# 128 rows per gather, node one-hots on ScalarE, earlier logits, and a mixing stage without GpSimd

## Chip, core and metric

The kernel runs on one core of a Trainium2 chip. The metric is the device time of one execution in microseconds (us). A core has a matrix engine (TensorE, PE in the rows, its weight loads PEld), a vector engine (VectorE, DVE), a scalar engine (ScalarE, ACT), GpSimd (POOL) and SyncE (SP). Each runs its own instruction queue in order and meets the others through semaphores. Everything is float32.

## What is computed

A two-layer graph block on 3125 nodes of 256 features and 50000 edges, sorted by destination. Cut to what matters here:

```python
# layer 0: two attention convolutions with one head (GATv2)
h      = leaky_relu(xl[src] + xr[dst] + edge_attr @ We, 0.2)
logits = h @ att
ex     = exp(logits - segment_max(logits, dst)[dst])
out    = segment_sum(xl[src] * (ex / segment_sum(ex, dst)[dst])[:, None], dst)

# layer 1: one attention convolution with eight heads
e   = leaky_relu(eh[src] + ee + et[dst], 0.2)
ex  = exp(e - segment_max(e, dst)[dst])
rst = segment_sum(ft[src] * (ex / segment_sum(ex, dst)[dst])[:, :, None], dst)

# layer 1: linear mixing, N = 3125
k2 = l2_normalize(k*k / (sum(k*k) + 1e-7), over nodes)
q2 = l2_normalize(q*q / (sum(q*q) + 1e-7), over features)
out = (v + q2 @ (k2.T @ v) / sqrt(N)) @ W_out + b_out
```

Beside them stand a four-layer linear attention, two mixtures of experts, and norms, which the change leaves alone.

## The kernel before

Nodes lie in 25 tiles of P = 125 partitions, edges in steps of 125. The function `messages` makes one convolution. It is called three times: calls 1 and 2 have one head (`one` is true), call 3 has eight. Its 432 steps form 27 groups of G = 16, and buffers over groups form a ring of RB = 3.

For each step it fetches the source rows of 125 edges with one indirect DMA from GpSimd (`gather`, L656), in four blocks of four steps; block b of group g waits until PE has summed the same block of group g - 3 (L653), whose rows it overwrites. A one-hot matrix `oht` (node by edge) gives PE the destination's term: SyncE loads a row of tile-relative numbers into all partitions (L673), and `node_hots` (L694) turns the 125 x 2000 block of a group into ones and zeros with one VectorE comparison. PE multiplies it with the node rows and, with one head, adds the gathered rows through an identity (`score`, L862 and L866; L872 with eight heads). VectorE makes the `relu` and its sum (L701, one head) and the `logits` (L709, or L718 to L722), running maxima (`own_maxima`, `carries`, `maxima`), and the exponent's `arguments` (L760 to L766); ScalarE makes the exponentials (L950), with one head the scaling of the gathered rows (L971), and the other one-hot `oh` (edge by node), step by step through a ring of four (L960, L964). With eight heads VectorE scales the rows (`scale`, L773). PE sums them with `oh` into one of three banks (`aggregate`, L908), and VectorE adds the bank to the accumulator (`combine`, L792), which it rescales once per group (`rescale`, L783 or L786).

Every engine runs a `body(j, ...)` per group, written out by hand. In body j the logits of group j get their maxima and exponentials, group j + 1 is scored, and group j - 1 is summed and combined. VectorE goes through k = 0 to 15: each k combines one step, with the maxima at k = 1, 3 and 5, the arguments at k = 8, the node one-hots of group j + 2 and the indices of group j + 3 at k = 9, the scaling at 12 to 15 (eight heads), and the logits of group j + 1 at the end. PE goes through eight pairs p, each with two scores and two sums, and five asides on p = 0 to 4: `turn_logits` (L879), `turn_ends` (L884, L885), `turn_carries` (L891), `turn_run` (L897), `spread_factor` (L902). ScalarE takes, per group, the exponentials, the scaling, and `edge_hots` of the next group (L960, L964).

`square_mix` makes the linear mixing. In its first loop over the 25 tiles PE projects, ScalarE squares, VectorE evicts and normalises (L1825 to L1843) and closes the convolution of call 3: it multiplies the accumulator (L1846) and adds it to `x2` (L1849). GpSimd adds the two column sums `ksum` and `k2sum` (L1635, L1644) and the bias `shift` to `x2` (L1640). In its second loop PE makes the output products (L1704) and VectorE adds them to `x2` (L1867).

## Time and profile before

| | us |
|---|---|
| median of 3 runs (lowest, highest) | 5218.85 (5206.32, 5223.74) |
| the profiled execution | 5204.3 |
| its span, from first to last instruction | 5202.5 |
| call 1 of `messages`, first to last gather | 1613.2 to 2291.2 |
| call 2 | 2537.1 to 3212.1 |
| call 3 | 3903.3 to 4594.3 |
| `square_mix` | about 4640 to 4812 |

| engine | busy us | share of the span |
|---|---|---|
| PE | 4340.8 | 83% |
| DVE | 2738.6 | 53% |
| ACT | 2171.7 | 42% |
| POOL | 2022.1 | 39% |

A row of a group names line, engine, operation, output and inputs with their shapes, and the count of instructions; then their busy time, the mean of one, and the idle time of the engine just ahead of them with what ended it. A PE operation in float32 is issued as two instructions, so sixteen steps are 32 rows. Idle time put down to "issue" is ended by nothing that the profile shows. The chain of work that ended last reaches only over the last part of the program and doesn't touch these stages, so they are read by windows.

### The profile page before, as it was taken

The page shows a single profiled execution, that of the slowest core. Times are in us where ns is not written, and L with a number is a line of the kernel's source. Part 1 is how long each engine was busy: PE and PEld are TensorE (multiplying, and loading weights), DVE is VectorE, ACT ScalarE, POOL GpSimd, SP SyncE. Part 2 cuts the span into 40 slices and gives each one's busy share as a digit, 9 for nine tenths or more (in the row PEclk, how much of TensorE's full clock was granted, in tenths as well). Part 3 has the DMA queues.
Part 4 walks back from the last instruction along what each step waited for, and adds up shares of the span by engine and source line. Part 5 has one row for each costly group of instructions (what it writes and reads, how often), then busy time and mean ns, then how long its engine had stood idle before and what let it go on. Part 6 is the DMA issues. An engine that isn't in the chain of part 4 may idle for free. (4 is left out here: it accounts for less than half of the span.)

```text
span 5202.5 us, 73734 instructions
## 1 busy us (share of the span) xinstructions
PE 4340.8 (83%) x21745; PEld 3584.4 (69%) x21746; DVE 2738.6 (53%) x8592; ACT 2171.7 (42%) x6651; POOL 2022.1 (39%) x1623
## 2 busy tenths in 40 slices
PE   9589999999995899988699998749936888878694
PEld 8478879788794777765577776438935666655694
DVE  2263452634523666764366666363355777766324
ACT  2243434434442666652366666122243333333222
POOL 0000000000004888840488885106618888833141
PEclk9789999999997999996899999659965666579697
DMA  5510000000005555530455553472267656620613
GB/s 141 145 52 10 18 10 1 18 10 18 1 21 124 126 126 125 125 88 19 98 125 127 129 125 83 93 219 68 63 146 151 136 135 135 134 67 25 202 36 87
DMA packets 364626, 463.24 MB, mean 89 GB/s; under 512 B 166429, under 2 KB 296743, under 8 KB 363790
## 3 DMA queue, kind: packets, MB, share of 16 engines
q1 hardware_dynamic: 172546, 258.16, 19.5%
q0 software_dynamic: 191744, 200.92, 17.5%
q8 instruction: 172, 2.82, 0.2%
q14 instruction: 164, 1.34, 0.1%
HBM read 396.61 MB, written 60.67 MB: 88 GB/s over the span
## 5 line engine op out<-in xcount | busy, mean ns | idle before, releaser
L656 POOL DMA_INDIRECT msg_rows<-tab_d,msg_cur x1296 | 1649.9, 1273 | 1762.8 <-DVE msg_cur L142 1368.7
L908 PE MATMUL msg_agp<-msg_rows,msg_oh 125*125 125x261 f32 (+2 forms) x2592 | 849.5, 457 | 14.3 <-DVE ga_acc L792 10.7
L908 PEld LDWEIGHTS msg_agp<-msg_rows,msg_oh 125*125 125x125 f32 x2592 | 549.0, 223 | 125.1 <-DVE ga_acc L792 18.2
L862 PE MATMUL msg_zp<-g_xr,msg_oht 127*125 x1728 | 544.3, 396 | 64.5 <-DVE msg_oht L696 64.2
L866 PE MATMUL msg_zp<-msg_rows,c_ident 125*125 125x256 f32 x1728 | 528.9, 387 | 81.9 <-DMA msg_rows<-tab_d,msg_cur 81.5
L701 DVE SCALAR_TENSOR_TENSOR msg_hid<-msg_zp,g_att 125x256 f32<-125x256 f32 x864 | 360.8, 420 | 334.3 <-PE msg_zp L866 329.5
L960 ACT ACTIVATE msg_dist<-c_iota,c_rel 125x125 f32<-125x125 f32 x1296 | 493.3, 387 | 49.7 <-PEq L3077 34.7
L964 ACT ACTIVATE msg_oh<-msg_dist,c_ones 125x125 f32<-125x125 f32 x1296 | 493.5, 387 | 0.0
L950 ACT ACTIVATE msg_ex<-msg_arg 125x16 f32<-125x16 f32 (+1 forms) x81 | 20.0, 247 | 984.9 <-DVE msg_delta L766 984.9
L866 PEld LDWEIGHTS msg_zp<-msg_rows,c_ident 125*125 125x125 f32 x1728 | 323.9, 190 | 153.7 <-DMA msg_rows<-tab_d,msg_cur 103.6
L792 DVE TENSOR_TENSOR gv_acc<-gv_acc,msg_agp 125x261 f32 (+1 forms) x864 | 364.4, 422 | 72.4 <-PE msg_agp L908 64.9
L862 PEld LDWEIGHTS msg_zp<-g_xr,msg_oht 127*125 127x125 f32 x1728 | 306.8, 189 | 117.1 <-issue 65.4
L1240 PE MATMUL mix_pb<-mix_ht,mix_w 128*128 128x125 f32 x3200 | 373.5, 275 | 0.0
L1249 PE MATMUL mix_pc<-mix_w,mix_ut 128*125 128x256 f32 x1600 | 361.8, 380 | 7.1 <-ACT mix_ut L1381 7.1
L1240 PEld LDWEIGHTS mix_pb<-mix_ht,mix_w 128*128 128x128 f32 x3200 | 365.6, 192 | 0.4
L971 ACT ACTIVATE msg_rows<-msg_rows,msg_ex 125x257 f32<-125x257 f32 x864 | 354.2, 497 | 1.8
L1516 DVE TENSOR_TENSOR mix_t<-mix_pc,mix_b 125x256 f32<-125x256 f32 x100 | 42.5, 425 | 543.5 <-PE mix_pc L1249 543.5
L1249 PEld LDWEIGHTS mix_pc<-mix_w,mix_ut 128*125 128x125 f32 x1600 | 292.9, 188 | 48.0 <-issue 8.3
L1202 PE MATMUL mix_pb<-mix_wp,mix_ht 128*125 128x256 f32 x1200 | 284.8, 389 | 4.3 <-ACT mix_ht L1321 4.3
L792 DVE TENSOR_TENSOR ga_acc<-ga_acc,msg_agp 125x264 f32 x432 | 184.2, 426 | 161.7 <-PE msg_agp L908 145.4
L1202 PEld LDWEIGHTS mix_pb<-mix_wp,mix_ht 128*125 128x125 f32 x1200 | 223.8, 193 | 36.9 <-issue 5.6
L1321 ACT ACTIVATE mix_ht<-mix_pa,mix_gb 128x125 f32<-128x125 f32 x208 | 83.0, 451 | 368.8 <-PE mix_pa L1191 368.8
(552 smaller groups left out, 7221.1 us busy)
## 6 DMA issues: line engine op xcount, KB each, us to landing
msg_oht<-rel_d SPq DMA_DIRECT2D x81, 875.0 KB
msg_rows<-tab_d,msg_cur POOLq DMA_INDIRECT x1296, 3.9
pl_raw<-in_edge_attr SPq DMA_DIRECT2D x25, 448.0 KB
msg_pens<-pen_d SPq DMA_DIRECT2D x270, 31.2 KB
msg_oht<-rel_d SPq DMA_DIRECT2D x81, 101.6 KB
mix_w<-in_L_mix_W SPq DMA_DIRECT2D x8, 1024.0 KB
m0w_wr<-in_L_ffn_w SPq DMA_DIRECT2D x16, 512.0 KB
m0w_w2r<-in_L_ffn_w SPq DMA_DIRECT2D x16, 512.0 KB
```

The lines of the kernel that those rows point to most:

```text
L656: nc.gpsimd.indirect_dma_start(out=rows[:, q, k, :], out_offset=None, in_=table, in_offset=bass.IndirectOffsetOnAxis(ap=cur[:, q, k:k + 1] ...
L701: last = nc.vector.scalar_tensor_tensor(out=hid[:, k, :], in0=zp[:, pair_bank(u, k // 2), (k % 2) * D:(k % 2 + 1) * D], scalar=0.0, in1=at ...
L792: nc.vector.tensor_tensor(a_t, a_t, agp[:, sum_bank(u, k), 0:AW], ALU.add).then_inc(combined.sem, 1)
L862: nc.tensor.matmul(z, hots, d_t, start=True, stop=False)
L866: last = nc.tensor.matmul(z, c.ident[0:P, 0:P], rows[:, u % RB, k, 0:D], start=False, stop=True)
L908: nc.tensor.matmul(agp[:, sum_bank(u, k), 0:AW], oh[:, u % RB, k, :], rows[:, u % RB, k, 0:AW], start=True, stop=True).then_inc(summed.sem, 1)
L960: nc.scalar.activation(dist[:, k % 4, :], c.iota[0:P, 0:P], ACT.Abs, scale=-1.0, bias=c.rel[:, bass.ds(g * G + k, 1)]).then_inc(dist_ready ...
L964: last = nc.scalar.activation(oh[:, u % RB, k - 1, :], dist[:, (k - 1) % 4, :], ACT.Relu, scale=-1.0, bias=c.ones[0:P, 0:1])
L971: nc.scalar.activation(r, r, ACT.Copy, scale=ex[:, u % RB, k:k + 1]).then_inc(scaled.sem, 1)
L1202: last = nc.tensor.matmul(pb[bank][0:P, lo:lo + D], ht[:, t % HR, kc, :], wp[:, w, kc, :], start=(kc == 0), stop=(kc == 1))
L1240: last = nc.tensor.matmul(out, w1[:, kc, f * 128:(f + 1) * 128], ht[:, t % HR, kc, :], start=(kc == 0), stop=(kc == 1))
L1249: last = nc.tensor.matmul(pc[t % 2][0:P, 0:D], ut[:, t % 2, f, :], w2[:, f, :], start=(f == 0), stop=(f == FC - 1))
```

## The change

The diff has five parts.

1. A gather fetches 128 rows: `rows` and `cur` get 128 partitions, and so does `src_s`, whose rows 125 to 127 stay zero, so that three more copies of table row 0 land in partitions that nothing reads.
2. `node_hots` moves from VectorE to ScalarE and becomes two activations over the 125 x 2000 block, |part - x| and relu(1 - |.|), the second of which waits for the first. It stands at the head of ScalarE's body, for group j + 2.
3. The `rescale` of the one-head calls takes its factor as a second tensor input and not as a scalar.
4. With eight heads PE makes all 16 scores of group j + 1 in pairs 0 to 3, four to a pair, and VectorE makes the logits of group j + 1 at k = 10 and not after k = 15.
5. `square_mix` has no GpSimd block. VectorE makes the two column sums in the first loop; the additions to `x2` (accumulator, then `shift`) move to the second loop, two tiles ahead of their use.

```diff
-        rows = st.sb("rows", [P, RB, G, TW])
-        cur = st.sb("cur", [P, RB, G], I32)
+        rows_all = st.sb("rows", [ROWS, RB, G, TW])
+        rows = rows_all[0:P]
+        cur = st.sb("cur", [ROWS, RB, G], I32)
...
-                            nc.gpsimd.indirect_dma_start(out=rows[:, q, k, :], out_offset=None, in_=table,
+                            nc.gpsimd.indirect_dma_start(out=rows_all[:, q, k, :], out_offset=None, in_=table,
...
-                def node_hots(g, u, lap):
-                    dve.wait_ge(hots_landed[u % RB].sem, hots_landed[u % RB].at(lap * hots_in + hots_in))
-                    nc.vector.tensor_scalar(oht[0:P, u % RB], oht[0:P, u % RB], c.part[0:P, 0:1], None, ALU.is_equal).then_inc(oht_ready.sem, 1)
...
-                        ch(nc.vector.tensor_scalar(a_t, a_t, fac[:, u % RB, 0:1], None, ALU.mult))
+                        ch(nc.vector.tensor_tensor(a_t, a_t, fac[:, u % RB, 0:1].broadcast_to([P, W]), ALU.mult))
...
                         if k == 9 and not final and spare:
-                            node_hots(j + 2, u + 2, i + (u + 2) // RB)
                             take_sources(j + RB, u)
+                        if not one and not final and k == 10:
+                            logits(j + 1, u + 1, i + (u + 1) // RB)
...
-                    if not final:
+                    if one and not final:
                         logits(j + 1, u + 1, i + (u + 1) // RB)
...
-                        if not final:
+                        if not final and one:
                             for k in (2 * p, 2 * p + 1):
                                 score(j + 1, u + 1, k, nts[k % (G // 2)], i + (u + 1) // RB)
+                        if not final and not one and p < PAIRS // 2:
+                            if p % 2 == 0:
+                                nts = node_tiles(j + 1, p // 2)
+                            for k in range(4 * p, 4 * p + 4):
+                                score(j + 1, u + 1, k, nts[k % (G // 2)], i + (u + 1) // RB)
...
+                def node_hots(g):
+
+                    act.wait_ge(hots_landed[g % RB].sem, hots_landed[g % RB].at((g // RB + 1) * hots_in))
+                    h = oht[0:P, g % RB]
+                    nc.scalar.activation(h, h, ACT.Abs, scale=-1.0, bias=c.part[0:P, 0:1]).then_inc(far_ready.sem, 1)
+                    act.wait_ge(far_ready.sem, far_ready.at(g + 1))
+                    nc.scalar.activation(h, h, ACT.Relu, scale=-1.0, bias=c.ones[0:P, 0:1]).then_inc(oht_ready.sem, 1)
...
                 def body(j, u, final=False):
+                    if j + 2 < NG:
+                        node_hots(j + 2)
                     weights(j, u)
...
-            @block.gpsimd
...
+                def sums(t):
...
+                    nc.vector.tensor_tensor(ksum[:], ksum[:], kk[:, t % R], ALU.add).then_inc(kk_summed.sem, 1)
+                    nc.vector.tensor_tensor(k2sum[:], k2sum[:], k2[:, t % R], ALU.add).then_inc(k2_summed.sem, 1)
...
                 for t in range(NT):
+                    if t + 2 < NT:
+                        base(t + 2)
+                    dve.wait_ge(x2_ready.sem, x2_ready.at(t + 1))
                     dve.wait_ge(out_done.sem, out_done.at(t + 1))
```

**PE, call 3, the middle of a body.** `msg_zp` is written by the scores, `msg_agp` by the sums; L897 is `turn_run`, L902 `spread_factor`. Before:

```order
L897 MATMUL msg_m<-c_ident,msg_run 125x128
L136 TENSOR_LOAD c_nt_row
L872 ISA
L872 MATMUL msg_zp<-ga_et,msg_oht 125x8
L872 ISA
L872 MATMUL msg_zp<-ga_et,msg_oht 125x8
L908 MATMUL msg_agp<-msg_rows,msg_oh 125x264 x2
L902 MATMUL msg_m<-msg_delta,msg_oh 125x8
L872 ISA
L872 MATMUL msg_zp<-ga_et,msg_oht 125x8
```

After (L895 is `turn_run`, L900 `spread_factor`, L906 the sums, L870 the scores):

```order
L870 MATMUL msg_zp<-ga_et,msg_oht 125x8
L870 ISA
L870 MATMUL msg_zp<-ga_et,msg_oht 125x8
L906 MATMUL msg_agp<-msg_rows,msg_oh 125x264 x2
L895 MATMUL msg_m<-c_ident,msg_run 125x128
L906 MATMUL msg_agp<-msg_rows,msg_oh 125x264 x2
L900 MATMUL msg_m<-msg_delta,msg_oh 125x8
L906 MATMUL msg_agp<-msg_rows,msg_oh 125x264 x6
L137 TENSOR_LOAD c_nt_row
```

The second half of the body holds sums alone, and the scores stand ahead of `turn_run`.

**VectorE, call 3.** Before, the last two scalings and combines of a body, and the logits (`msg_lg`) behind them:

```order
L792 TENSOR_TENSOR ga_acc<-ga_acc,msg_agp 125x264
L773 TENSOR_TENSOR msg_rows<-msg_rows,msg_ex 125x4x264
L792 ISA
L792 TENSOR_TENSOR ga_acc<-ga_acc,msg_agp 125x264
L773 TENSOR_TENSOR msg_rows<-msg_rows,msg_ex 125x4x264
L718 TENSOR_TENSOR msg_lg<-msg_zp,msg_rows 125x16x8
L721 TENSOR_TENSOR msg_lg<-msg_lg,ga_ee 125x128
L722 SCALAR_TENSOR_TENSOR msg_lg<-msg_lg 125x128
L136 TENSOR_LOAD c_nt_row
```

After, from the arguments' last instruction at k = 8 on (L791 combines, L717 to L721 are the logits):

```order
L765 TENSOR_SCALAR msg_delta<-msg_delta,c_link 1x8
L791 ISA
L791 TENSOR_TENSOR ga_acc<-ga_acc,msg_agp 125x264
L143 TENSOR_SCALAR msg_cur<-c_src_s 128x16
L791 ISA
L791 TENSOR_TENSOR ga_acc<-ga_acc,msg_agp 125x264
L717 TENSOR_TENSOR msg_lg<-msg_zp,msg_rows 125x16x8
L720 TENSOR_TENSOR msg_lg<-msg_lg,ga_ee 125x128
L721 SCALAR_TENSOR_TENSOR msg_lg<-msg_lg 125x128
L791 ISA
L791 TENSOR_TENSOR ga_acc<-ga_acc,msg_agp 125x264
```

The logits stand ahead of five combines and four scalings, and the comparison over `msg_oht` that stood between L792 and the copy to `msg_cur` is gone from VectorE.

**ScalarE, call 1, from one group's edge one-hots to the next exponential.** After (before, the rows on `msg_oht` aren't there):

```order
L967 ACTIVATE msg_oh<-msg_dist,c_ones 125x125 x2
L974 ACTIVATE msg_oht<-msg_oht,c_part 125x2000
L976 ACTIVATE msg_oht<-msg_oht,c_ones 125x2000
L953 ACTIVATE msg_ex<-msg_arg 125x16
L982 ACTIVATE msg_rows<-msg_rows,msg_ex 125x257 x4
```

Two wide activations now stand ahead of the exponential that `scale` and the next sums need.

## Rows read from the trace of the kernel before

**Rows 1.** Windows (us, busy us and count by engine, PE clock, DMA share, GB/s).

```profile
1640.00:2266.00 626.00, 574.66 (x2685) 457.12 (x2685) 421.98 (x1800) 385.06 (x1200) 504.31 (x400) 0.99 0.55 125
2562.00:3187.00 625.00, 575.46 (x2698) 460.20 (x2697) 418.04 (x1781) 385.03 (x1200) 503.09 (x401) 0.99 0.55 125
3929.00:4569.00 640.00, 535.83 (x1863) 408.39 (x1863) 447.18 (x1118) 233.93 (x816) 518.33 (x400) 0.60 0.61 134
...
4680.00:4710.00 30.00, 24.42 (x92) 14.51 (x92) 28.04 (x66) 17.97 (x75) 17.91 (x24) 1.00 0.00 1
```

**Rows 2.** Timeline, call 1, POOL (start, duration, instruction, idle before and releaser).

```profile
1713.87 1.21 POOL L656 DMA_INDIRECT msg_rows<-tab_d,msg_cur  x1 [0.30 <-issue]
1715.39 2.12 POOL L656 DMA_INDIRECT msg_rows<-tab_d,msg_cur  x1 [0.30 <-issue]
```

**Rows 3.** Groups by line, call 1, 1640 to 2266 us.

```profile
L656 POOL DMA_INDIRECT msg_rows<-tab_d,msg_cur x400 | 505.1, 1263 | 121.9 <-issue 115.2 <-PE msg_agp L908 6.7
...
L696 DVE TENSOR_SCALAR msg_oht<-msg_oht,c_part 125x2000 f32<-125x2000 f32 x24 | 30.5, 1269 | 0.0
```

**Rows 4.** Waits, call 1, same stretch (who waited for whom, us, times, longest).

```profile
PE msg_zp L866 <- DMA msg_rows<-tab_d,msg_cur: 27.3, 20, 2.5
...
PE msg_m L902 <- DVE msg_delta L766: 23.5, 24, 1.4
```

**Rows 5.** Lines L656 and L328 (ns min/median/max), and the landing of L656.

```profile
L656 POOL DMA_INDIRECT msg_rows<-tab_d,msg_cur x1296: 1210/1214/2244, 1613.2 to 4593.1; - x186
...
DMA to landing us min/median/max: 3.8/3.9/15.6
...
L328 POOL DMA_INDIRECT pl_got<-etab_d,pl_idx x4: 1000/1002/1177, 43.2 to 47.3; - x4
```

**Rows 6.** Timeline, call 1, ACT.

```profile
1715.35 0.22 ACT L950 ACTIVATE msg_ex<-msg_arg 125x16 f32<-125x16 f32 x1 [10.74 <-DVE msg_delta L766]
...
1740.57 0.22 ACT L950 ACTIVATE msg_ex<-msg_arg 125x16 f32<-125x16 f32 x1 [9.14 <-DVE msg_delta L766]
```

**Rows 7.** Groups by line and form, whole span: wide activations, the rescale of call 3.

```profile
L971 ACT ACTIVATE msg_rows<-msg_rows,msg_ex 125x257 f32<-125x257 f32 x864 | 354.2, 497 | 1.8
...
L2946 ACT ACTIVATE cp_up<-gv_acc 125x1280 f32<-125x1280 f32 x5 | 6.4, 1282 | 8.6 <-DVEq L2939 8.6
...
L786 DVE TENSOR_TENSOR ga_acc<-ga_acc,msg_fac 125x264 f32 x27 | 11.7, 433 | 15.4 <-issue 15.4
```

**Rows 8.** Groups by line, call 3, 3929 to 4569 us.

```profile
L656 POOL DMA_INDIRECT msg_rows<-tab_d,msg_cur x400 | 518.7, 1297 | 121.9 <-issue 99.7 <-PE msg_agp L908 22.2
...
L773 DVE TENSOR_TENSOR msg_rows<-msg_rows,msg_ex 125x1056 f32<-125x1056 f32 x96 | 119.7, 1249 | 0.0
```

**Rows 9.** Waits, call 3, same stretch.

```profile
PE msg_m L879 <- DVE msg_lg L722: 88.3, 25, 16.6
...
DVE msg_lg L718 <- DMA msg_rows<-tab_d,msg_cur: 15.9, 2, 8.6
```

**Rows 10.** Groups by line, `square_mix`, DVE, 4680 to 4710 us.

```profile
L1846 DVE TENSOR_TENSOR ga_acc<-ga_acc,sq_zero 125x256 f32<-125x256 f32 x8 | 7.6, 945 | 0.0
L1849 DVE TENSOR_TENSOR sq_x<-sq_x,ga_acc 125x256 f32<-125x256 f32 x8 | 6.7, 835 | 0.3
L1843 DVE TENSOR_SCALAR ga_ee<-sq_sq,sq_rec,sq_qn 125x256 f32<-125x256 f32 x8 | 5.3, 660 | 0.3
```

**Rows 11.** Timeline, `square_mix`, DVE: one tile of the first loop, then the second loop.

```profile
4702.32 0.68 DVE L1825 TENSOR_TENSOR sq_qk<-sq_pq,sq_bq 125x512 f32<-125x512 f32 x1
...
4706.38 0.68 DVE L1825 TENSOR_TENSOR sq_qk<-sq_pq,sq_bq 125x512 f32<-125x512 f32 x1
...
4768.62 0.42 DVE L1867 TENSOR_TENSOR sq_x<-sq_x,sq_pq 125x256 f32<-125x256 f32 x1 [4.59 <-PE sq_pq L1704]
...
4772.87 0.42 DVE L1867 TENSOR_TENSOR sq_x<-sq_x,sq_pq 125x256 f32<-125x256 f32 x1 [1.30 <-PE sq_pq L1704]
4774.59 0.42 DVE L1867 TENSOR_TENSOR sq_x<-sq_x,sq_pq 125x256 f32<-125x256 f32 x1 [1.31 <-PE sq_pq L1704]
```

More of the change, by code:

```diff
@@ L22 @@
 EVEN = 112
+ROWS = 128
 NT = N // P
@@ L413, in _ @@
                 dve.sem_inc(pens_ready.sem, 1)
-                take(1, c.src_s[:, 0:S], bank[0][0:P, 0:S])
+                take(1, c.src_s[0:P, 0:S], bank[0][0:P, 0:S])
                 take(2, c.last[:], bank[1][0:P, 0:S])
@@ L613, in messages @@
         dist_ready = st.sem("dist_ready")
+        far_ready = st.sem("far_ready")
         z_ready = st.sem("z_ready")
@@ L912, in body @@
                     for p in range(PAIRS):
-                        if not final and p % (PAIRS // 2) == 0:
+                        if not final and one and p % (PAIRS // 2) == 0:
                             nts = node_tiles(j + 1, p // (PAIRS // 2))
-                        if not final:
+                        if not final and one:
                             for k in (2 * p, 2 * p + 1):
+                                score(j + 1, u + 1, k, nts[k % (G // 2)], i + (u + 1) // RB)
[3 more added lines that the diff above has]
+                            for k in range(4 * p, 4 * p + 4):
                                 score(j + 1, u + 1, k, nts[k % (G // 2)], i + (u + 1) // RB)
@@ L983, in body @@
                         edge_hots(j + 1, u + 1)
+                node_hots(0)
                 edge_hots(0, 0)
+                node_hots(1)
                 body(0, 0)
@@ L1574, in square_mix @@
         xk = [st.ps(f"xk{j}", [128, D]) for j in range(2)]
-        order, pool_order = st.sem("order"), st.sem("pool_order")
+        order = st.sem("order")
         w_in, v_in, small_in = st.sem("w_in"), st.sem("v_in"), st.sem("small_in")
@@ L1816, in _ @@
                 nc.vector.tensor_copy(bvc[:], bv[:].unsqueeze(2).broadcast_to([128, 2, P])).then_inc(bvc_ready.sem, 1)
+                nc.vector.memset(k2sum[:], 0.0)
+                nc.vector.memset(ksum[:], 0.0)
                 ch(nc.vector.tensor_scalar(zero[:], d, 0.0, None, ALU.is_equal))
@@ L1819, in _ @@
                 ch(nc.vector.reciprocal(zero[:], d))
+                ch(nc.vector.tensor_tensor(shift[:], bq[:, 2], bias[:], ALU.add))
                 def evict(t):
@@ L1857, in _ @@
                         queries(i - LP - 2)
-                    if LP + 4 <= i:
-                        closed(i - LP - 4)
+                    if LP + 3 <= i < NT + LP + 3:
+                        sums(i - LP - 3)
+                    if i < NT + LP:
+                        closed(i - LP)
                 dve.wait_ge(kn_rooted.sem, kn_rooted.at(1))
@@ L1863, in _ @@
                 nc.vector.tensor_scalar_mul(kn[:], kn[:], ROOT).then_inc(kn_ready.sem, 1)
-                dve.wait_ge(x2_ready.sem, x2_ready.at(NT))
+                dve.wait_ge(bvo_ready.sem, bvo_ready.at(1))
+                ch(nc.vector.tensor_tensor(shift[:], shift[:], bvo[:], ALU.add))
+                dve.wait_ge(closed_ready.sem, closed_ready.at(NT))
+                for t in range(2):
+                    base(t)
                 for t in range(NT):
+                    if t + 2 < NT:
+                        base(t + 2)
+                    dve.wait_ge(x2_ready.sem, x2_ready.at(t + 1))
                     dve.wait_ge(out_done.sem, out_done.at(t + 1))
@@ L3104, in program @@
         c.iota_low = st.sb("iota_low", [P, 16])
-        c.nt_row, c.src_s = st.sb("nt_row", [1, S], I32), st.sb("src_s", [P, S + G], I32)
+        c.nt_row, c.src_s = st.sb("nt_row", [1, S], I32), st.sb("src_s", [ROWS, S + G], I32)
         c.rel, c.last, c.eas = st.sb("rel", [P, S]), st.sb("last", [P, S]), st.sb("eas", [P, S, 2])
```

39 lines of the change are left out of this document (12 added, 27 removed).

## The prediction

> **What bounds the kernel now.** I read four views: the windows for each engine's busy time and the clock by stage, the timeline of GpSimd, the groups by line for prices, and the waits for what each engine lacked. The chain of waits reaches only over the end of the program and says nothing here.
>
> The three calls of `messages` are paced by GpSimd. Its gathers stand one behind the other, 1.21 us each and 0.30 us apart [rows 2]; over 400 gathers of call 1 it is busy 505.1 us and idle 121.9 us, 0.305 us a gather [rows 3], so that even a wait that is put down to PE costs no more than the usual gap. A group of 16 takes 16 x (1.263 + 0.305) = 25.1 us, and the window has 626.00 / 25 = 25.04 us a group [rows 1]. PE is close behind: 574.66 us busy in that window, 23.0 us a group [rows 1], and its waits for a gather's landing come to 27.3 / 25 = 1.1 us a group, those of `spread_factor` for VectorE to 23.5 / 25 = 0.94 us [rows 4]. Call 2 reads the same to a microsecond [rows 1].
>
> Call 3 has 640.00 / 25 = 25.6 us a group [rows 1], and GpSimd again fills it: 16 x (1.297 + 0.305) = 25.6 us [rows 8]. Here PE is at a mean granted clock of 0.60, against 0.99 in calls 1 and 2 [rows 1], is busy 21.4 us a group and waits 88.3 / 25 = 3.5 us a group for the logits [rows 9]. VectorE waited for a gather there only twice [rows 9], so PE with VectorE is as slow as GpSimd, and both must get faster for the call to gain.
>
> In `square_mix` VectorE bounds the first loop: 28.04 of 30 us busy [rows 1], 4.06 us a tile [rows 11]. In the second loop PE does, 1.72 us a tile, with VectorE idle 1.3 us of it [rows 11].
>
> **The gather's price.** No row has a gather of 128 rows. The nearest have 125 rows, 1.214 us, and 108 rows, 1.002 us (L328, whose rows are longer) [rows 5]. A straight line through both has 12.5 ns a row and 1.25 us at 128, my upper end; but it gives -0.35 us at no rows, so the step between them can't be the price of the rows alone. With any fixed part of zero or more, growth from 108 rows ends between 1.00 and 1.19 us. I take 1.00, the row that it starts from, because a fixed part of most of the price would leave the rows little; the lower end is a little below it, 0.98. What is special to 125 I can't see in a row. The Trainium skill (DMA: Bandwidth & Descriptors, "Why a DMA increments its semaphore by 16 and not by 1") says that a DMA is split over the largest number of engines up to 16 that divides its outer dimension: 5 for 125 rows, 12 for 108, 16 for 128. If the price follows the rows per engine (25, 9, 8), a line through the two measured ones gives 0.99 us at 128, an estimate; no run here shows it yet, and the sum would be the same.
>
> **Locks on GpSimd.** One gather in call 1 takes 2.12 us where its neighbours take 1.21 [rows 2]; the mean is 1.263 against a median of 1.214 [rows 3, 5], 0.049 x 16 = 0.78 us a group. In each group one VectorE instruction is of a kind by itself, the comparison of 125 x 2000, 1.27 us [rows 3]; I put the loss down to it. In call 3 the loss is 0.083 x 16 = 1.33 us a group [rows 8]; the scaling of four steps, two tensor inputs in SBUF and 1.25 us long [rows 8], stands there too and stays. I give it half, 0.66 us.
>
> The rescale of calls 1 and 2 becomes an instruction with two SBUF inputs, as that of call 3 is at 0.43 us [rows 7]. If each held up a gather for its whole length, 54 x 0.43 = 23 us would go to GpSimd. The Trainium skill (SBUF — State Buffer, "Who interferes with whom") says just this, that an instruction with two SBUF inputs contends with a GpSimd instruction that reads SBUF. By that rule the sum stays what it is, since 0.43 us a group fits in the slack that GpSimd gets below. In time on VectorE the edit costs under 0.1 us a group, beside PE's work.
>
> **Calls 1 and 2.** GpSimd then needs 16 x (1.00 + 0.305) = 20.9 us a group, and is no longer the bound. PE is: 25.04 - 1.1 = 23.9 us, its busy time and the wait of `spread_factor`, which nothing here removes. Any gather below 1.19 us leaves it so (16 x (1.19 + 0.305) = 23.9), which is why this term hardly hangs on the price. ScalarE gets two passes over 2000 elements per row. From 497 ns at 257 and 1282 ns at 1280 elements [rows 7], 0.77 ns an element, a pass is 1.83 us, two with the wait between them 3.9 us. They stand ahead of the exponential, behind which the scaling, PE's sums and, by the freed rows, the gathers are queued. From one exponential to the next ScalarE is idle 9.14 of 25.2 us [rows 6], so its work is 16.1 us and becomes 20.0 us, under 23.9. The cover is 3.9 us; without it each pass would add its length to the group. VectorE loses the comparison and isn't bound. From group 0 to 26 there are 26 paces: 2 x 26 x (25.04 - 23.9) = **-59 us**. The low end is PE without its wait either, 23.0 us, -106 us; the high end is the unchanged price below.
>
> **Call 3.** GpSimd: 20.9 + 0.66 = 21.5 us. PE: with all scores in the first half and the logits at k = 10, the matrix transpose of the logits (L879) finds them ready; 25.6 - 3.5 = 22.1 us, if the clock stays at 0.60. The second half of the body has sums alone. VectorE has there seven combines of 0.43, four scalings of 1.25 and the logits of some 1 us, about 9 us, and stays ahead enough: three banks let PE run on into the next body's scores. Queued behind the moved logits are five combines and the scalings; they now wait if group j + 1 hasn't landed, half a body earlier than before. With a gather of 20.9 us in a ring of three groups it has. I add 0.2 us and take 22.3: 26 x (25.6 - 22.3) = **-86 us**. Ends: 21.5 us, GpSimd's own, -107 us; no gain at all.
>
> **Starts.** Ahead of the first pace each call gathers a whole group: 16 x 0.21 = 3.4 us less, three times, partly covered by the loads that land then: **-8 us**. ScalarE's first node one-hots finish some 3 us later than VectorE's did, before the first rows land.
>
> **`square_mix`.** Per tile VectorE loses the addition to `x2` (about 0.8) and gets two sums at 0.43. The accumulator's product falls from 0.95 to 0.43 and L1843 from 0.66 to some 0.35, if their length comes from GpSimd [rows 7, 10]: 4.06 - 0.8 + 0.86 - 0.52 - 0.31 = 3.3 us. PE is busy 24.42 / 30 x 4.06 = 3.3 us a tile, so 3.5 us for both together, 25 x 0.56 = **-14 us**. In the second loop VectorE has three additions, 1.3 us, under PE's 1.72; the two tiles ahead of it lie in the wait of 4.59 us [rows 11]. Were it not for the contention, the first loop would keep 4.06 + 0.06 us, no gain.
>
> **Sum.** 59 + 86 + 8 + 14 = 167 us off the profiled execution's 5204.3: 5037. That execution lies 14.6 us below the median of the three runs, so I forecast 5037 + 14 = 5051, rounded to **5050 us**, 3.2% below.
>
> **Rivals.**
> *The gather isn't cheaper* (1.21 us at 128 rows too, the price being one of each instruction). For it speaks only that rows of 125 are so steady, against it the 1.00 us of 108. Then the locks alone go: 52 x 0.78 = 41 us, in call 3 GpSimd at 16 x 1.519 + 0.66 = 25.0, 26 x 0.6 = 17 us, and 14 in the mixing: 5204 - 72 + 15 = 5147. Chance 0.12.
> *Call 3 keeps its pace*: PE's halves get uneven, sums in the second wait for banks behind VectorE's scalings while the clock stays at half. 5050 + 86 = 5136. Chance 0.10. Against it: PE's wait of 3.5 us was the largest there.
> *Everything reaches its floor*: 106 + 107 + 10 + 18 = 241 us, 4978. Chance 0.12; it needs a higher clock in call 3, which less idle time may give.
> *Slower: the gather is dearer at 128 rows.* The place is GpSimd, where 1296 gathers stand in a row. It eats the other 72 us at 72 / 1296 = 0.055 us, so from 1.27 us on. At 1.30 us it would be 1296 x 0.086 - 72 = +39 us, 5258. For it: three more rows, all fetching the same address, and the straight line to 1.25. Chance 0.05.
> The likeliest case, that of the sum, has 0.61.
>
> **Range and chances.** 4985 to 5160 takes in the first two rivals (5147 and 5136) with some room, and leaves out the slower one and most of the floor, 0.17 together. A measurement of this kernel can tell about 0.3% from no change (15 us). Faster by more 0.93, within 0.03 (a gather at 1.26 to 1.28 us), slower 0.04.
>
> **What would show it.** In the profile after: the gather's median at or below 1.05 us and waits of GpSimd above 0.30 us (it isn't the bound); PE's waits for landings near zero and a pace of 23.9 us in calls 1 and 2; in call 3 no wait of L879's successor for the logits and a pace near 22; ScalarE's idle time ahead of the exponential down to some 4 us in calls 1 and 2; 3.5 us a tile in the mixing. I am wrong if the gather costs 1.2 us or more, if ScalarE is late at the exponential, or if PE in call 3 waits for its banks.

## The result: 3.3% less on the chip of record, and 5.9% more on another

The changed kernel took 5043.47 us (median of 4, 5022.84 to 5056.19), the kernel before 5214.91 us on the same chip: a ratio of 0.9667, 95% interval 0.963 to 0.9705. The profiled execution has a span of 5021.0 us against 5202.5. The forecast of 5050 us holds for that chip. The experiments ran on five chips. On the first of them, where the changed kernel itself wasn't run, its variants behaved as on the chip of record. On the other four every kernel with gathers of 128 rows was 3.7 to 8.4% slower than the kernel before (the 8.4% has pauses added), the changed kernel itself, which ran on one of them, 5.9% (5509.19 us against 5202.58), while the kernel before stayed within 0.4% of its time. Each chip was seen once, so the runs don't tell a lasting property of a chip from a condition of that hour; "kind of chip" below stands for either. Both are results of this case. First the chip of record.

| stage (us, from its first to its last instruction) | before | after |
|---|---|---|
| `messages`, call 1 | 718.1 | 667.6 |
| `messages`, call 2 | 710.6 | 666.5 |
| `messages`, call 3 | 736.5 | 676.1 |
| `square_mix` | 162.9 | 143.6 |
| `mix_layers`, not touched | 1317.7 | 1310.0 |

The four touched stages lost 174.3 us, where the sum had 167. Another 7.7 us came off `mix_layers`, which the change leaves alone; over the traces of this case that stage takes 1309.8 to 1317.8 us whatever the edit, so they are no gain of the change.

Windows of the kernel after: a stretch of 21 groups of call 1, one of 19 groups of call 3, and 30 us of the first loop of `square_mix` (columns as in [rows 1]).

```profile
1713.00:2210.00 497.00, 478.43 (x2286) 387.56 (x2286) 334.00 (x1507) 416.12 (x1090) 320.95 (x336) 1.00 0.53 136
3951.00:4404.00 453.00, 405.87 (x1462) 290.34 (x1461) 320.45 (x857) 257.71 (x684) 309.94 (x304) 0.66 0.56 147
4520.00:4550.00 30.00, 30.00 (x121) 18.91 (x120) 27.44 (x97) 23.16 (x97) 0.00 (x0) 1.00 0.00 1
```

The pace is 497 / 21 = 23.67 us a group in call 1 (25.04 before) and 453 / 19 = 23.84 in call 3 (25.6). GpSimd is busy 65% of the first window where it was at 81% [rows 1]. PE is busy 96% of it, and every microsecond of the one in `square_mix`.

The gather in the kernel after: line L659 over the whole span (ns min/median/max, then who waited for it), and the groups of call 1 and of call 3, to set against [rows 3, 5, 8].

```profile
L659 POOL DMA_INDIRECT msg_rows<-tab_d,msg_cur x1296: 941/949/2030, 1609.6 to 4427.2; - x186
...
  DVE msg_lg L717: 28.6, 3
  PEld msg_zp L864: 11.8, 6
  PE msg_zp L864: 8.8, 5
```

```profile
L659 POOL DMA_INDIRECT msg_rows<-tab_d,msg_cur x336 | 321.4, 957 | 176.5 <-issue 102.4 <-PE msg_agp L906 74.1
```

```profile
L659 POOL DMA_INDIRECT msg_rows<-tab_d,msg_cur x304 | 309.9, 1020 | 142.8 <-issue 77.2 <-PE msg_agp L906 65.7
```

A gather of 128 rows takes 0.949 us where one of 125 took 1.214. Its mean in call 1 lies 8 ns above the median (49 ns before): the stretched gather of each group is gone with the comparison. GpSimd is idle 0.53 us a gather, not 0.305, and it is PE's sums that it waits for: it has stopped being the bound. PE's matmuls waited for a landing 5 times in the whole program, 20 times in one call before [rows 4].

Waits of the kernel after, first the window of call 1, then that of call 3.

```profile
ACT msg_ex L953 <- DVE msg_delta L765: 79.5, 21, 3.8
...
PE msg_m L900 <- DVE msg_delta L765: 18.6, 21, 0.9
```

```profile
PEld msg_agp L906 <- DVE ga_acc L791: 60.4, 88, 1.7
PE msg_agp L906 <- DVE ga_acc L791: 30.3, 41, 1.3
```

ScalarE still has 79.5 / 21 = 3.8 us a group to spare ahead of the exponential. In call 3 the wait of 3.5 us a group for the logits [rows 9] has no row any more, but PE waits 30.3 / 19 = 1.6 us a group for VectorE to add up a bank of sums.

ScalarE in one group of call 1 of the kernel after (timeline): the two passes and the exponential behind them, with its idle time.

```profile
1903.53 1.95 ACT L974 ACTIVATE msg_oht<-msg_oht,c_part 125x2000 f32<-125x2000 f32 x1
1905.52 1.96 ACT L976 ACTIVATE msg_oht<-msg_oht,c_ones 125x2000 f32<-125x2000 f32 x1
1911.27 0.22 ACT L953 ACTIVATE msg_ex<-msg_arg 125x16 f32<-125x16 f32 x1 [3.79 <-DVE msg_delta L765]
```

### The profile page after: what moved, and what is told of

Same layout as the page of the kernel before. It is cut to its first block and busy times, and to the rows that moved or that the text cites. A ratio compares the mean times of both kernels' runs of the same rounds, so it can differ in the third digit from the quotient of the medians.

```text
span 5021.0 us, 73791 instructions
## 1 busy us (share of the span) xinstructions
PE 4288.0 (85%) x21745; PEld 3539.8 (70%) x21746; DVE 2621.2 (52%) x8590; ACT 2480.5 (49%) x6813; POOL 1578.0 (31%) x1544
## 5 line engine op out<-in xcount | busy, mean ns | idle before, releaser
L659 POOL DMA_INDIRECT msg_rows<-tab_d,msg_cur x1296 | 1265.0, 976 | 1966.8 <-DVE msg_cur L143 1360.7
L906 PE MATMUL msg_agp<-msg_rows,msg_oh 125*125 125x261 f32 (+2 forms) x2592 | 820.6, 445 | 56.5 <-DVE ga_acc L791 45.3
L906 PEld LDWEIGHTS msg_agp<-msg_rows,msg_oh 125*125 125x125 f32 x2592 | 523.1, 214 | 191.5 <-DVE ga_acc L791 87.8
L700 DVE SCALAR_TENSOR_TENSOR msg_hid<-msg_zp,g_att 125x256 f32<-125x256 f32 x864 | 360.7, 420 | 337.5 <-PE msg_zp L864 330.5
L864 PE MATMUL msg_zp<-msg_rows,c_ident 125*125 125x256 f32 x1728 | 518.9, 381 | 8.8 <-DMA msg_rows<-tab_d,msg_cur 8.8
L791 DVE TENSOR_TENSOR gv_acc<-gv_acc,msg_agp 125x261 f32 (+1 forms) x864 | 364.4, 422 | 71.0 <-PE msg_agp L906 64.0
L864 PEld LDWEIGHTS msg_zp<-msg_rows,c_ident 125*125 125x125 f32 x1728 | 324.7, 188 | 63.6 <-DMA msg_rows<-tab_d,msg_cur 11.8
L791 DVE TENSOR_TENSOR ga_acc<-ga_acc,msg_agp 125x264 f32 x432 | 184.3, 427 | 163.0 <-PE msg_agp L906 144.9
```

Source lines behind the costliest of these rows:

```text
L659: nc.gpsimd.indirect_dma_start(out=rows_all[:, q, k, :], out_offset=None, in_=table, in_offset=bass.IndirectOffsetOnAxis(ap=cur[:, q, k:k ...
L700: last = nc.vector.scalar_tensor_tensor(out=hid[:, k, :], in0=zp[:, pair_bank(u, k // 2), (k % 2) * D:(k % 2 + 1) * D], scalar=0.0, in1=at ...
L791: nc.vector.tensor_tensor(a_t, a_t, agp[:, sum_bank(u, k), 0:AW], ALU.add).then_inc(combined.sem, 1)
L864: last = nc.tensor.matmul(z, c.ident[0:P, 0:P], rows[:, u % RB, k, 0:D], start=False, stop=True)
L906: nc.tensor.matmul(agp[:, sum_bank(u, k), 0:AW], oh[:, u % RB, k, :], rows[:, u % RB, k, 0:AW], start=True, stop=True).then_inc(summed.sem, 1)
```

## Experiments on a chip like that of record

Four kernels ran beside the kernel before (5209.28 us there). All of them compute the whole result.

**125 rows again, the rest of the change kept.**

```diff
-ROWS = 128
+ROWS = 125
```

> The changed kernel with 125 rows a gather again, all else kept. Theory (the gather's price falls with 128 rows): the price goes back from 0.95 to 1.21 us, GpSimd needs 16 x 1.52 = 24.3 us a group and bounds calls 1 and 2 again (23.7 us now), the first three groups of each call cost 4.3 us more each, call 3 gets about 0.6 us a group longer: some 80 us more than the changed kernel, 0.983 of before. Rival (the comparison that left VectorE brought most of it): the price stays near 1.0 us or the time stays within 20 us of the changed kernel, 0.967 to 0.971.

Measured: 5126.66 us, ratio 0.9829 (0.9791 to 0.9867). The gather is back at 1.211 us with GpSimd idle 0.305 us behind each, so that it bounds all three calls at 24.25, 24.25 and 24.77 us a group; they took 693.7, 693.5 and 711.8 us. With the comparison off VectorE hardly a gather of calls 1 and 2 is stretched (5 of 864 by over 60 ns): their mean is 1211 ns. So what the change does apart from the rows is worth 1.7%.

**The kernel before with gathers of 128 rows, nothing else.**

```diff
-        rows = st.sb("rows", [P, RB, G, TW])
-        cur = st.sb("cur", [P, RB, G], I32)
+        rows_all = st.sb("rows", [ROWS, RB, G, TW])
+        rows = rows_all[0:P]
+        cur = st.sb("cur", [ROWS, RB, G], I32)
```

> The kernel before with 128 rows a gather and nothing else. Theory: the price falls to 0.95 us here too, with the comparison on VectorE still stretching one gather a group; calls 1 and 2 gain 40 to 50 us each since PE bounds them then, call 3 gains only its start (about 10 us), since PE with VectorE was as slow as GpSimd there: 0.980 to 0.983 of before. Rival (the parts only work together): under 40 us in all, 0.992 or more.

Measured: 5108.35 us, 0.9815 (0.9787 to 0.9843): calls 669.2, 666.2 and 722.8 us. Calls 1 and 2 have all of their gain from the rows alone. Call 3 has a third of it (736.5 to 722.8), for there PE still waits for the logits, as the waits of this kernel show in call 3, 3951 to 4404 us:

```profile
PE msg_m L881 <- DVE msg_lg L724: 52.7, 18, 3.1
```

That is 2.9 us a group. The two halves of the change seem to add up, 0.9829 x 0.9815 = 0.965 against 0.967 for both, but by stages they don't, and the match in the whole is luck. In calls 1 and 2 the rest alone gains 24 and 17 us, the rows alone 49 and 44, and both together only 51 and 44: once PE is the bound, what frees GpSimd further is worth nothing. In call 3 the rest gains 25, the rows 14, and both together 60: there each needs the other.

**One-hots of the nodes back on VectorE.**

```diff
+                def node_hots(g, u, lap):
+                    dve.wait_ge(hots_landed[u % RB].sem, ...)
+                    nc.vector.tensor_scalar(oht[0:P, u % RB], oht[0:P, u % RB], c.part[0:P, 0:1], None, ALU.is_equal)
...
-                    if j + 2 < NG:
-                        node_hots(j + 2)
```

> The changed kernel with the comparison for the node one-hots back on VectorE at k = 9. Theory: with gathers of 0.95 us GpSimd has idle time, so that a stretched gather costs nothing; calls 1 and 2 stay within 5 us each; in call 3 the comparison adds 1.3 us to VectorE's busiest stretch, where PE waits for banks: 20 to 35 us longer. Together 0.967 rises to 0.970 to 0.975. Rival (the lock on GpSimd still counts): 0.8 us a group in all three calls, 60 us, 0.979.

Measured: 5039.61 us, 0.9672 (0.9642 to 0.9701), which can't be told from the changed kernel's 0.9667 on the chip of record; I had expected 0.970 to 0.975. Gathers are stretched again in call 1, their mean is 1019 ns where it was 957:

```profile
L659 POOL DMA_INDIRECT msg_rows<-tab_d,msg_cur x337 | 343.5, 1019 | 154.3 <-issue 103.3 <-PE msg_agp L913 51.0
```

but GpSimd has slack now, and the pace of call 1 is 23.7 us a group in both. Calls 1 and 2 took 673.3 and 668.2 us, call 3 683.0, 7 us more where I had 20 to 35. Call 3 also tells what the new order is worth: 722.8 us in the kernel before with 128 rows, 683.0 here, 40 us.

**What sets the price of a gather.** Calls 1, 2 and 3 fetch 126, 127 and 125 rows.

```diff
+        fetched = (126, 127, 125)[call]
+        rows_all = st.sb("rows", [ROWS, RB, G, TW])[0:fetched]
```

> The changed kernel with 126 rows a gather in call 1, 127 in call 2 and 125 in call 3. Theory (the price follows the rows that one DMA engine gets, with the largest divisor up to 16 as the number of engines: 9, 127 and 25): about 1.0 us in call 1, 2.4 to 2.7 us in call 2, 1.21 us in call 3; call 2 then takes 43 to 48 us a group. Rival (the price follows the rows alone, or 128 is a special case): 1.2 us in all three calls, all near 24.3 us a group.

Measured: 5773.76 us in a single execution, call 2 alone 1375.6 us; call 1 with 126 rows took 668.0 us, as with 128. The groups of GpSimd in a stretch of call 1 and of call 2:

```profile
L660 POOL DMA_INDIRECT msg_rows<-tab_d,msg_cur x386 | 385.6, 999 | 174.4 <-issue 108.1 <-PE msg_agp L907 66.3
```

```profile
L660 POOL DMA_INDIRECT msg_rows<-tab_d,msg_cur x324 | 826.1, 2550 | 177.8 <-issue 177.8
```

The medians are 997 ns for 126 rows, 2548 for 127, 1211 for 125, beside 949 for 128 and 1002 for 108 [rows 5]. The largest number up to 16 that divides these is 14, 1, 5, 16 and 12, and the rows for each are 9, 127, 25, 8 and 9: the price follows them, 0.84 us and 13.4 ns for each row (0.95 at 8, 0.96 at 9, 1.18 at 25, 2.55 at 127; the measured ones lie within 0.04). That a gather is split this way can be counted in the DMA packets of the traces: one of 128 rows leaves 32 packets of four rows; one of 126 28 of four and 14 of one; one of 125 30 of four and 5 of one; one of 127 31 of four and one of three. These are 16 queues with 8 rows each, 14 with 9, 5 with 25 and one with 127. The trace agrees with the Trainium skill (DMA: Bandwidth & Descriptors, "Why a DMA increments its semaphore by 16 and not by 1"), which has this rule for the engines that a DMA is split over. Of the five numbers tried, 127, a prime, is the dearest by far.

## Experiments on chips of the other kind

**Four single edits.** They ran together on a second chip of the experiments, the kernel before at 5231.9 us beside them.

Call 3 in the old order:

```diff
-                        if not one and not final and k == 10:
-                            logits(j + 1, u + 1, i + (u + 1) // RB)
...
-                        if not final and not one and p < PAIRS // 2:
...
+                        if not final:
                             for k in (2 * p, 2 * p + 1):
```

> The changed kernel with call 3 in the order of before: two scores to each of PE's eight pairs, the logits after k = 15. Theory (the earlier logits took PE's wait of 3.5 us a group and gave 1.6 to 3 us of it back to the wait for banks): PE waits for the logits again, the pace of call 3 goes from 23.7 to about 25.2 us, 35 to 45 us longer, 0.974 to 0.975 of before. Rival (call 3 gained by the gathers alone): no difference over 10 us.

`square_mix` as before the change, with its sums and the base on GpSimd:

> The changed kernel with the mixing stage of before, GpSimd's block included. Theory: the stage takes 163 us again instead of 144, 19 us longer in all, 0.970 to 0.971 of before, and VectorE's products of the accumulator are back at 0.95 us each. Rival (the gain of the stage came from elsewhere, as the clock): under 8 us.

The last two of the four scalings of call 3 one body later:

```diff
-                        if not one and k in (12, 13, 14, 15):
-                            scale(j, u, k - 12)
+                        if not one and k in (12, 14):
+                            scale(j, u, (k - 12) // 2)
+                        if not one and not first and k in (2, 6):
+                            scale(j - 1, u - 1, (k + 6) // 4)
...
```

> The changed kernel with VectorE's four scalings of call 3 spread out: blocks 0 and 1 at k = 12 and 14, blocks 2 and 3 at k = 2 and 6 of the next body. Theory (what PE still waits for in call 3 is a bank behind VectorE's scalings, 1.6 us a group and more ahead of its weight loads): the wait goes, the pace falls from 23.7 to 22.0 to 22.7 us, 25 to 45 us less, 0.958 to 0.962 of before. Rival (PE's own work at its granted clock is the bound, the waits would only move): within 10 us of the changed kernel.

The factor of calls 1 and 2 spread one pair of steps later on PE, and eight steps scaled ahead of it on ScalarE:

```diff
-                        if p == 4:
+                        if p == (5 if one else 4):
...
-                        for k in range(4):
+                        for k in range(8):
```

> The changed kernel with the aside of the factor in calls 1 and 2 one pair later on PE (p = 5) and ScalarE's factor after eight scalings, not four. Theory (PE bounds calls 1 and 2 and idles 0.9 us a group ahead of this aside, waiting for VectorE): that idle time goes, 23.65 falls to 22.8 us a group, 35 to 45 us less in both calls, 0.958 to 0.960 of before. Rival (PE then waits for VectorE at the next scores or sums): less than 10 us.

Measured: 5570.32 us (1.0632, 1.0579 to 1.0686), 5581.12 (1.0662, 1.0616 to 1.0707), 5519.86 (1.055, 1.0498 to 1.0603), 5430.25 (1.0369, 1.0327 to 1.0411). All four miss what every theory said, and by stages the excess is in the message calls alone: 875, 868 and 791 us with the old order; 868, 865 and 800 with the old mixing stage; 872, 865 and 758 with later scalings; 801, 805 and 809 with the later factor. The second of them has the same calls as the changed kernel, 667.6, 666.5 and 676.1 us on the chip of record, so its edit can't be what makes them slow. What can still be read is the stage that isn't disturbed: `square_mix` took 162.9 us in its old form and 142.0 to 144.5 in the three others, beside each other, which confirms 19 us for that part. With GpSimd's block back, VectorE's product of the accumulator takes 945 ns and the scaling of the queries 610 again. Beside the second kernel, whose calls are the changed kernel's, the later factor takes 67 and 60 us off calls 1 and 2, and the later scalings 42 us off call 3. What they bring on a chip like the first stays open.

**The changed kernel again, and the old order again**, together on a third chip.

> The changed kernel itself, nothing edited. It is here because four kernels that ran together on another chip (call 3 in the old order, the mixing stage in the old form, later scalings, a later factor) took 5430 to 5581 us, while the kernel before took 5232 us beside them, and all of the excess lay in the three message calls. The kernel with the old mixing stage has the same three calls as the changed kernel, and they took 868, 865 and 800 us there against 667.6, 666.5 and 676.1 us. Theory A: the excess belongs to that chip and to gathers of 128 rows, not to the edits; this run then gives either 5040 us (ratio 0.967) on a chip like the first, or about 5570 us (ratio 1.06) on one like the other, and the kernel beside it moves with it. Theory B: the edits brought it; this run gives 5040 us while the old order of call 3 beside it gives about 5570 us on the same chip.

> The changed kernel with call 3 in the old order: its scores two a pair of steps through the group and its logits at the group's end, as before the change; calls 1 and 2 untouched. The same kernel as the run that took 5570 us beside a kernel before of 5232 us. Theory A (the chip): ratio to the changed kernel beside it near 1. My prediction priced the old order's wait of PE for the logits at 3.5 us a group; the trace of the changed kernel shows 1.6 us a group of new waits for sum banks in its place, so the order by itself should be worth (3.5 - 1.6) x 27 = 51 us: 5094 us where the changed kernel takes 5043. Rival (the order is worth nothing once gathers are short): within 15 us of the changed kernel.

Measured: 5509.19 us, 1.0592 (1.0551 to 1.0633), and 5511.4 us, 1.0605 (1.056 to 1.0649), the kernel before at 5202.58. The kernel without any edit is slow as well, and the old order stays beside it: theory A. The calls took 852.0, 851.3 and 773.4 us; with the old order call 3 took 777.8, so here the order is worth 4 us (and on the second chip -9, 791 us against 800), where it was worth 40 on the other kind of chip.

Windows of this second trace of the changed kernel, call 1 and call 3, to set against those above:

```profile
1713.00:2210.00 497.00, 425.48 (x1815) 333.06 (x1813) 267.81 (x1200) 331.07 (x865) 253.44 (x267) 0.90 0.42 107
4300.00:4753.00 453.00, 371.95 (x1331) 266.64 (x1331) 290.35 (x774) 237.56 (x634) 284.93 (x276) 0.65 0.51 133
```

Nobody is the bound: in 497 us GpSimd issues 267 gathers where it issued 336, and each engine is busy less. A gather costs 0.946 us as before. The timeline of call 1 shows where the time is. The line is: start, duration, instruction, idle time before it and what ended it.

```profile
1894.46 0.59 PE L864 MATMUL msg_zp<-msg_rows,c_ident 125*125 125x256 f32 x2
...
1895.78 0.27 PE L877 MATMUL msg_m<-c_ident,msg_lg 125*16 125x125 f32 x1
...
1898.00 0.95 POOL L659 DMA_INDIRECT msg_rows<-tab_d,msg_cur  x1 [0.30 <-issue]
...
1900.32 0.42 DVE L700 SCALAR_TENSOR_TENSOR msg_hid<-msg_zp,g_att 125x256 f32<-125x256 f32 x1 [4.69 <-remote]
...
1903.23 0.94 POOL L659 DMA_INDIRECT msg_rows<-tab_d,msg_cur  x1 [4.29 <-PE msg_agp L906]
```

PE's pair of scores (L864) is over at 1895.05 by its record and the transpose of the logits (L877) at 1896.05. VectorE's L700 needs only that pair, and goes on at 1900.32; "remote" says that the event which released it belongs to no recorded instruction. The trace's semaphore events say the same: the increment behind L877 comes 14 ns after the matmul's end in all 27 groups of call 1 on the chip of record, and here in 24 of 27 groups more than 1 us after it, 4.3 us in the median. In the group shown, six instructions of PE ended between 1895.06 and 1898.22, and none of their increments is recorded before 1900.2.

Below, this is the hold. The increments that the gathers make themselves thin out too: 2257 of the 6912 of call 1 are recorded, and 6891 of them on the chip of record. GpSimd, which runs ahead, issues until its own wait for PE's sums (4.29 us in the last row); the others go on 1.4 us after its last gather ended. In 23 of the 24 held groups of call 1 the increment comes within 0.22 us of the moment at which the rows of that last gather have landed, by the DMA packets of the trace. So in call 1 the hold ends with the stream of gathers. In call 3, where increments come up to 8 us late, some are released in the midst of one.

The transfers themselves aren't slower: rows land 2.46 us after a gather's start here and 2.47 us on the chip of record, in the median of call 1, which leaves slower DMA or memory out as the cause. PE then has also lost its clock, which is granted at 0.90 in the mean where it was 1.00. A group takes 29.7 us instead of 23.7.

**Three ways to gather, one a call.** Call 1 is the control, call 2 limits the gathers under way to eight, call 3 has 125 rows. The whole result is computed.

```diff
+        fetched = (128, 128, 125)[call]
+        window = (False, True, False)[call]
...
+                        if window and uu >= 0:
+                            pool.wait_ge(landed[uu % RB][bb].sem, ...)
```

> The changed kernel with a different gather in each message call: call 1 as it is (128 rows), call 2 with 128 rows and one wait more on GpSimd (before a block of four gathers it waits until the block two before it has landed, so that at most eight gathers are under way), call 3 with 125 rows. Background: the changed kernel took 5043 us on the first chip and 5509 us (calls 852, 851, 773 us) on a later one, where the kernel before took 5203 us. In the slow trace TensorE's semaphore increments come up to 4.4 us after the end of the matmul that makes them, once in every group, while gathers are issued back to back, and only 2375 of the 6912 increments that the gathers of call 1 make are recorded, against 7019 in the trace of the first chip. Call 1 is the control: 667 us tells a chip like the first, about 850 us one like the other. Theory A (back-to-back gathers of 128 rows hold up all semaphore increments on such a chip): on a chip of the slow kind call 3 takes 712 us, as with 125 rows on the fast kind, not 773 to 800 us, and call 2 is shorter than call 1 if the limit keeps the gathers from piling up (700 us or less). Theory B (the one-hots on ScalarE or the ring of four are at fault): call 3 stays at 770 to 800 us on a slow chip although its gathers are of 125 rows, and call 2 equals call 1. On a chip of the fast kind: 667, 667 to 675 and 712 us.

Measured, on a fourth chip: 5445.32 us, 1.046 (1.043 to 1.0491); calls 852.5, 854.3 and 711.0 us. Groups of GpSimd in call 1 and call 3 of this kernel:

```profile
L665 POOL DMA_INDIRECT msg_rows<-tab_d,msg_cur x320 | 306.9, 959 | 315.7 <-PE msg_agp L912 224.6 <-issue 86.2 <-remote 4.9
```

```profile
L665 POOL DMA_INDIRECT msg_rows<-tab_d,msg_cur x326 | 403.1, 1237 | 99.3 <-issue 89.2 <-PE msg_agp L912 10.0
```

The control says that the chip is of the other kind. Call 3 with 125 rows takes 711.0 us on it, as on the first kind (711.8), where 128 rows take 758 to 809: it is the gather of 128 rows, and not the passes on ScalarE, the ring of four or the order, all of which stand in that call. Theory B has fallen. The limit in call 2 says little, because it hardly ever acts: idle time of GpSimd is ended by a landing once in that call (5.1 us, at its start), and at a gather's start only one earlier gather is still under way in the median, by the DMA packets. A limit that bites wasn't tried. But the number under way can't be all of it, since in call 3 two are in the median, more than in call 1. Call 3 isn't free of it, only unharmed: 4641 of its 6912 increments are recorded, where it was 6876 with 125 rows on the first kind, and the increment behind the transpose comes after 14 ns in all 22 groups that have it.

**126 rows, and pauses.** Call 1 is the control again, call 2 has 126 rows, call 3 has 128 with a pause ahead of each gather.

```diff
+        fetched = (128, 126, 128)[call]
...
+                            if pause is not None:
+                                ch(nc.gpsimd.memset(pause[:], 0.0))
```

> The changed kernel with a different gather in each message call: call 1 as it is (128 rows, the control), call 2 with 126 rows, call 3 with 128 rows and a pause on GpSimd before each (a MEMSET of 125x128 elements into a tile that nothing reads, and the wait for its end). Background: on a third chip of the slow kind, calls of 128 rows took 852 and 854 us and call 3 with 125 rows took 711.0 us, as on the fast kind (711.8 us), so gathers of 128 rows are what such a chip holds against this change. Two reasons are open. Theory R (rate): the hold-up needs a gather every 1.26 us; one every 1.52 us (125 rows) is slow enough. Then 126 rows (997 ns and 0.3 us of gap, one every 1.30 us) stay slow in call 2 (800 us or more where call 1 takes 850), and call 3 with pauses (a gather every 1.5 to 1.8 us) takes what GpSimd's pace gives, 16 x 1.5 to 1.8 us a group: 700 to 790 us, with TensorE's increments at once after its matmuls. Theory E (number of queues that carry rows: 16 or 14 against 5): call 2 stays slow too, but call 3 with its pauses stays held up: increments late by over 1.5 us in it. Theory K (only all 16 queues together do it): call 2 with 126 rows takes 670 to 690 us. On a chip of the fast kind: call 1 667 us, call 2 670 to 680 us, call 3 700 to 790 us.

Measured, on a fifth chip, again of the other kind: 5675.96 us, 1.0842 (1.0811 to 1.0873); calls 871.1, 850.9 and 930.5 us. Call 2 is held like call 1 (in 24 of 27 groups the increment behind the transpose is late, by 4.5 us in the median), so a split over 14 queues is no better than one over 16: theory K has fallen. The pause came out longer than meant; gathers follow each other at 1.96 us, as the timeline of GpSimd in call 3 shows:

```profile
4499.20 0.95 POOL L667 DMA_INDIRECT msg_rows<-tab_d,msg_cur  x1 [0.79 <-POOL msg_pause L665]
4500.16 0.22 POOL L665 MEMSET msg_pause<- 125x128 f32 x1
4501.16 0.99 POOL L667 DMA_INDIRECT msg_rows<-tab_d,msg_cur  x1 [0.79 <-issue]
```

16 x 1.96 = 31.4 us a group is what they cost by themselves, and the pace was 33.1. The hold on PE's increments is gone: the one behind the transpose comes after 14 ns in the 26 groups that have it, and 5814 of the gathers' 6912 are recorded. The 1.7 us a group beyond the pauses have no cause that I know. By the sign that stands in its own expectation (increments late by over 1.5 us in call 3) theory E has fallen too: 16 queues alone don't do it, the gathers must also follow each other fast. Whether the rate is all of it stays open, for no gather of 125 rows can come as often as every 1.25 us, and 128 rows every 1.5 us, which might keep most of the gain, wasn't tried.

## Why the forecast came out, step by step

**The gather's price** was the right choice of bound and a little too careful: 0.949 us against 1.00, below my lower end of 0.98. The straight line through 125 and 108 rows, which gave 1.25, failed because the price isn't one of the rows but of the rows for each of the queues; the reading with the divisor rule gave 0.99. So the 1.00 that I took rested on the wrong argument and came near by luck; the rule that I only named beside it was the right one.

**Locks.** 0.78 us a group for the comparison in calls 1 and 2: right, mean and median now differ by 8 ns. In call 3 I left 0.66 us and (1.020 - 0.949) x 16 = 1.1 us stayed. Neither counts for anything on the clock, since GpSimd isn't the bound, and the kernel with the comparison back on VectorE shows it. The rescale with two SBUF inputs does reach a gather, as the Trainium skill (SBUF — State Buffer, "Who interferes with whom") has it, by a third of its 0.43 us. (The same section tells of a probe in which such an instruction did not hold up a DMA; here it does.) Timelines of the kernel after, GpSimd and VectorE:

```profile
1898.10 1.08 POOL L659 DMA_INDIRECT msg_rows<-tab_d,msg_cur  x1 [0.30 <-issue]
1899.49 0.95 POOL L659 DMA_INDIRECT msg_rows<-tab_d,msg_cur  x1 [0.30 <-issue]
```

```profile
1897.94 0.43 DVE L782 TENSOR_TENSOR gv_acc<-gv_acc,msg_fac 125x257 f32 x1 [0.66 <-issue]
```

The gather that starts under it takes 0.13 us longer; one that has started before it doesn't. That happens in 20 of the 27 groups of call 1 and makes up most of the 8 ns of the mean.

**Calls 1 and 2.** From the end of the third group's sums to the last group's they lost 31.7 and 25.6 us, 57 together over 24 groups, where the sum had 59 over 26. The pace of 23.67 us is PE's own, as forecast at 23.9. ScalarE's passes are 1.95 and 1.96 us (1.83 in the estimate), and its idle time ahead of the exponential is 3.79 us where I had 3.9 of cover.

**Starts.** The term of 8 us was mis-sized: from the first gather to the end of the third group's sums call 1 gained 17.6, call 2 17.3 and call 3 11.8 us, 47 together. I priced one group ahead of the first pace. But the ring starts empty, and until it has filled the first three groups all run at the gather's own pace, which fell from 25 to 20 us.

**Call 3.** The term of 86 us was mis-sized the other way: 47 us by the same count. The pace is 23.84, not 22.3. The wait for the logits went, as the step said (3.5 us); but "stays ahead enough" was wrong: PE waits 1.6 us a group for banks behind VectorE's scalings. That is the mechanism of the second rival, in part. Starts and call 3 together were forecast at 94 us and gave 94, which is luck.

**`square_mix`** gave 19.3 us for 14. The product and the scaling of the queries fell to 0.42 and 0.41 us from the 0.95 and 0.66 of [rows 10], as the groups of VectorE of the kernel after, 4520 to 4550 us, show:

```profile
L1850 DVE TENSOR_TENSOR ga_acc<-ga_acc,sq_zero 125x256 f32<-125x256 f32 x10 | 4.2, 417 | 0.0
L1839 DVE TENSOR_SCALAR ga_ee<-sq_sq,sq_rec,sq_qn 125x256 f32<-125x256 f32 x10 | 4.1, 412 | 0.6 <-DVE sq_qn L1836 0.3
```

With GpSimd's block back they are 0.95 and 0.61 again, as said above, so it is the contention that went. PE, which I had beside VectorE at 3.3 us a tile, bounds it now; a tile takes 3.08 us, not 3.5, so 3.3 was too high for PE's own work.

**The range** rested on one trace from one chip. No rival had a chip on which the shorter gather holds up other engines' increments, and nothing in the trace before points to it: of the 6912 increments of its gathers in each call 6887 to 6904 are recorded. My rival on the slower side was a dearer gather, which is true of no gather of 128 rows here. With four of the five chips of the experiments of the other kind, 0.93 for faster was far too sure as a statement on this kernel. That it held is the luck of the chip.

## What to carry to other kernels

Price an indirect gather by its rows divided by the largest divisor up to 16 of their number, and pad a number of rows that divides badly; then ask at once who bounds the stage next, because here GpSimd's 5 us a group in call 1 became 1.4. Time such a change on several chips before it is kept: this one is worth 3.3% or costs 5.9%, and the version with 125 rows and all else of the change (1.7% faster on one kind) is the safer one, since its call 3 took no longer on the other kind; its calls 1 and 2 weren't tried there. When every engine is idle at once and a wait ends with nothing that the records name, compare the semaphore events with the ends of the instructions that make them.

## What the runs showed of the hardware that I had not expected

The chips used here differ in how soon an increment of a semaphore is seen under a stream of gathers. On the chip of record and on the first of the experiments it is seen after 14 ns nearly always. On the other four, with gathers of 126 or 128 rows every 1.25 to 1.3 us, it is seen over 4 us late in most groups of 16 of calls 1 and 2, when the last gather under way has landed, and up to 8 us late in call 3; and about two thirds of the gathers' own increments leave no record. Gathers of 125 rows every 1.52 us did no harm to the time in the one call that had them. What in the chip holds the increments, whether a chip keeps its kind, and whether the kernel before with 128 rows alone is held as well, no run here shows.

A gather of 127 rows costs GpSimd 2.55 us, of 128 rows 0.95. Moving 2000-element comparisons off VectorE frees GpSimd (1019 to 957 ns a gather), and was worth nothing that could be measured in the whole once gathers had 128 rows.
